# A macaron block on eight cores: the projection's loops are interchanged, and the softmax takes several PSUM banks per instruction

## The reference

```python
x = x + 0.5 * ffn(layernorm(x))
x = x + attn(layernorm(x))
x = x + 0.5 * ffn(layernorm(x))

def attn(x, Wkqv, bkqv, Wp, bp):          # 16 heads, D = 1024
    y = einsum('bnd,hde->bhne', x, Wkqv) + bkqv
    k, q, v = y[..., :1024], y[..., 1024:2048], y[..., 2048:]   # v has 64 columns
    A = einsum('bhnd,bhmd->bhnm', q, k) / sqrt(1024)
    A = softmax(where(causal, A, -inf))
    sa = einsum('bhnm,bhmd->bnhd', A, v).reshape(B, N, D)
    return sa @ Wp + bp
```

## Time and profile before

| | us |
|---|---|
| time, median of 2 runs | 8747.25 (8661.77 to 8832.72) |
| the profiled execution's own time | 8626.65 |
| its span, slowest core (core 4) | 8624.3 |
| TensorE matmul busy, core 4 | 5421.7 (63%) |
| TensorE weight load busy | 2495.0 (29%) |
| VectorE busy | 1917.7 (22%) |
| ScalarE busy | 1238.3 (14%) |

### The profile page before, as it was taken

How to read it: one execution, slowest core, us unless ns; L and a number is a source line. 1 busy time by engine, 2 the same in 40 slices (tenths; PEclk the granted TensorE clock), 3 DMA queues, 4 the chain that set the end, 5 groups by cost and what they waited for, 6 DMA issues and landing times.

```text
span 8624.3 us, 68745 instructions; the slowest of 8 cores (8527.9 to 8624.3 us)
## 1 busy us (share of the span) xinstructions
PE 5421.7 (63%) x24192; PEld 2495.0 (29%) x24192; DVE 1917.7 (22%) x4042; ACT 1238.3 (14%) x2572; POOL 176.0 (2%) x231
## 2 busy tenths in 40 slices
PE   4466465685766757667576675766757755446555
PEld 2122122232333323333233232332323322112222
DVE  2112121222221222222222222222222221210220
ACT  1112110111111111111111111111111111100110
POOL 0000000000000000000000000000000000000000
PEclk9677677776777868778688786887878877767777
DMA  3311313010101101011010010100101002322122
GB/s 68 56 23 36 59 20 52 11 21 0 21 5 16 18 3 21 5 16 21 1 21 10 11 21 1 21 10 11 21 0 21 1 1 90 72 50 33 38 46 42
DMA packets 170432, 213.87 MB, mean 25 GB/s; under 512 B 20816, under 2 KB 154224, under 8 KB 167792
## 3 DMA queue, kind: packets, MB, share of 16 engines
q0 software_dynamic: 154192, 155.24, 12.5%
q1 hardware_dynamic: 15904, 54.25, 1.8%
HBM read 339.49 MB, written 25.17 MB: 42 GB/s over the span
## 4 chain that ended last, share of the span: by engine, by line
PE 60%; DVE 15%; DMA 10%; issue 7%; ACT 6%; DVEq 1%; ACTq 0%; POOLq 0%; SPq 0%
PE psF L645 23%; PE psF L725 16%; PE psF L415 8%; PE psF L379 5%; ACT Pst L756 5%; DVE stat L743 5%; DMA f2b<-f 3%; PE psF L807 3%; DMA f2a<-f 3%; DVE PTs L791 2%; PE psT L786 2%; DVE Pst L777 2%; DVEq L74 1%; PE psF L336 1%; DMA f1b<-f 1%
## 5 line engine op out<-in xcount | busy, mean ns | idle before, releaser
L645 PE MATMUL psF<-ln_fm,wsl 128*128 128x512 bf16 x8704 | 1945.9, 388 | 41.7 <-DMA wsl<-wkqv 41.7
L725 PE MATMUL psF<-Kb,Qb 128*128 128x512 bf16 (+3 forms) x5120 | 1366.6, 439 | 0.0
L786 PE MATMUL psT<-ident,Pst 128*128 128x128 bf16 x2176 | 297.0, 300 | 1602.8 <-DVE Pst L777 1558.7
L645 PEld LDWEIGHTS psF<-ln_fm,wsl 128*128 128x128 bf16 x8704 | 870.5, 100 | 1112.2 <-issue 210.7
L725 PEld LDWEIGHTS psF<-Kb,Qb 128*128 128x128 bf16 x5120 | 570.7, 119 | 720.4 <-issue 463.5
L786 PEld LDWEIGHTS psT<-ident,Pst 128*128 128x128 bf16 x2176 | 198.6, 130 | 1755.1 <-issue 1755.1
L756 ACT ACTIVATE Pst<-psF,stat 128x512 bf16<-128x512 f32 (+3 forms) x640 | 398.7, 623 | 2122.4 <-DVE stat L747 2085.5
L668 ACT ACTIVATE Qb<-psF,bkqvq_sb 128x512 bf16<-128x512 f32 x512 | 351.7, 687 | 1423.6 <-PE psF L645 1423.5
L415 PE MATMUL psF<-mhb,f2b 128*128 128x512 bf16 x1024 | 350.5, 519 | 324.8 <-DMA f2b<-f 316.9
L415 PE MATMUL psF<-mha,f2a 128*128 128x512 bf16 x1024 | 347.6, 516 | 325.5 <-DMA f2a<-f 317.6
L657 DVE TENSOR_SCALAR Kb<-psF,bkqv_sb 128x512 bf16<-128x512 f32 x512 | 384.5, 751 | 630.2 <-PE psF L645 630.2
(11 more groups left out here) (106 smaller groups left out, 2252.0 us busy)
## 6 DMA issues: line engine op xcount, KB each, us to landing
wsl<-wkqv POOLq DMA_DIRECT2D x64, 1024.0 KB, 9.4
f2a<-f POOLq DMA_DIRECT2D x64, 512.0 KB, 5.3
f2b<-f POOLq DMA_DIRECT2D x64, 512.0 KB, 5.3
f1a<-f POOLq DMA_DIRECT2D x8, 1024.0 KB, 11.3
xta<-x SPq DMA_DIRECT2D x4, 2048.0 KB, 8.3
xs<-xta SPq DMA_DIRECT2D x4, 2048.0 KB, 6.5
x1t<-xs SPq DMA_DIRECT2D x4, 2048.0 KB, 9.1
xs<-x1t SPq DMA_DIRECT2D x4, 2048.0 KB, 7.6
```

What stands on the lines that cost most here:

```text
L645: outap=outap, ts=ts: e.matmul(outap, wsl[g][:, gw * c + 128 * jj: gw * c + 128 * jj + ofw], ln2_fm[:, 2048 * c + 512 * ts: 2048 * c + 512 ...
L725: lambda e, c=c, i=i, kw=kw, st=st, qb=qb: e.matmul(bank(st[i], kw), Qb[:, 2048 * c + 128 * qb: 2048 * c + 128 * (qb + 1)], Kb[:, 2048 * c ...
L786: (lambda e, col, i2=4 * tg + q, par=par: e.transpose(psT[:, col: col + 128], Pst[par][:, 128 * i2: 128 * (i2 + 1)], ident[:]))
```

## The change

Three edits, all in `build_program`:

1. In the projection, c is now the outer and ts the inner loop: the four banks are filled together, four matmuls in turn have the same weights, and the last matmul of each bank stands among the last four of the 32. One wait, at the first matmul of the tile, now names all four banks with their evictions in tile j-1, and only the last of the 32 matmuls counts up sT. The four evictions are written behind it.
2. The maximum (L743) and the exponential (L756) are taken over spans of several banks: one span of the whole W for even qb and for odd qb with W up to 1536, two spans (banks 3 to 5, and bank 0) for odd qb with W above 1536.
3. Where there is one span, its maximum is written negated straight into the column that the exponential reads, and its row sum straight into the column that the reciprocal reads: L747 and L767 are left out. The reciprocal waits for ScalarE as well.

```diff
-                        for ts in range(4):
-                            w = [("sW", wdone[g]),
-                                 ("sS", bankS[ts]), ("sV", bankV[ts])]
-                            if h == 0 and j == 0 and ts == 0:
-                                w += entry2
+                        w = [("sW", wdone[g])]
+                        for ts in range(4):
+                            w += [("sS", bankS[ts]), ("sV", bankV[ts])]
                             if j > 0:
                                 w.append(ev[(j - 1, ts)])
-                            for c in range(8):
+                        if h == 0 and j == 0:
+                            w += entry2
+                        for c in range(8):
+                            for ts in range(4):
...
-                                         waits=w if c == 0 else [],
-                                         inc="sT" if c == 7 else None)
-                            mmj = sch.cnt["sT"]
+                                         waits=w if (c == 0 and ts == 0) else [],
+                                         inc="sT" if (c == 7 and ts == 3) else None)
+                        mmj = sch.cnt["sT"]
+                        for ts in range(4):
...
+                    if par == 0:
+                        pieces = [(0, 0, W)]
+                    else:
+                        pieces = [(0, 1536, min(W, 1536))]
+                        if W > 1536:
+                            pieces.append((1536, 0, W - 1536))
+                    npc = len(pieces)
+                    if npc == 1:
+                        sch.emit("vector", lambda e, pc=pieces[0], par=par: e.reduce_max(
+                            stat[:, 26 + par: 27 + par],
+                            psF[:, pc[1]: pc[1] + pc[2]], AX, negate=True), inc="sV")
...
+                    for idx, pc in enumerate(pieces):
+                        acc = (smx[:, 8 + 2 * par: 9 + 2 * par] if npc == 1
+                               else smx[:, 4 * par + idx: 4 * par + idx + 1])
                         sch.emit("scalar",
...
+                                     psF[:, pc[1]: pc[1] + pc[2]], AF.Exp,
                                      bias=stat[:, 26 + par: 27 + par],
-                                     accum_out=smx[:, 4 * par + i: 4 * par + i + 1]),
+                                     accum_out=acc),
...
+                    if npc > 1:
+                        sch.emit("vector", lambda e, npc=npc, par=par: e.reduce_sum(
...
-                        waits=[("sV", ls_mark)], inc="sV")
+                        waits=[("sV", ls_mark), ("sS", expall)], inc="sV")
```

More of the change, by code:

```diff
@@ L632, in build_program @@
                         ofw = min(128, gw - 128 * jj)
+                        w = [("sW", wdone[g])]
                         for ts in range(4):
-                            w = [("sW", wdone[g]),
-                                 ("sS", bankS[ts]), ("sV", bankV[ts])]
-                            if h == 0 and j == 0 and ts == 0:
-                                w += entry2
+                            w += [("sS", bankS[ts]), ("sV", bankV[ts])]
                             if j > 0:
                                 w.append(ev[(j - 1, ts)])
-                            outap = (bank(ts) if ofw == 128
-                                     else psF[0:64, 512 * ts: 512 * ts + 512])
-                            for c in range(8):
+                        if h == 0 and j == 0:
+                            w += entry2
+                        for c in range(8):
+                            for ts in range(4):
+                                outap = (bank(ts) if ofw == 128
+                                         else psF[0:64, 512 * ts: 512 * ts + 512])
                                 sch.emit("tensor",
@@ new lines, in build_program @@
+                    npc = len(pieces)
[3 more added lines that the diff above has]
+                            psF[:, pc[1]: pc[1] + pc[2]], AX, negate=True), inc="sV")
+                    else:
+                        for idx, pc in enumerate(pieces):
+                            sch.emit("vector", lambda e, pc=pc, idx=idx: e.reduce_max(
+                                stat[:, 20 + idx: 21 + idx],
+                                psF[:, pc[1]: pc[1] + pc[2]], AX), inc="sV")
+                        sch.emit("vector", lambda e, par=par, npc=npc: e.reduce_max(
+                            stat[:, 26 + par: 27 + par], stat[:, 20: 20 + npc], AX,
+                            negate=True), inc="sV")
@@ L751, in build_program @@
                     mxd = sch.cnt["sV"]
-                    order = [3, 0, 1, 2] if nb == 4 else list(range(nb))
-                    for i in order:
-                        kw = min(512, W - 512 * i)
+                    for idx, pc in enumerate(pieces):
+                        acc = (smx[:, 8 + 2 * par: 9 + 2 * par] if npc == 1
+                               else smx[:, 4 * par + idx: 4 * par + idx + 1])
                         sch.emit("scalar",
-                                 lambda e, i=i, kw=kw, st=st, par=par: e.activation(
-                                     Pst[par][:, 512 * i: 512 * i + kw],
-                                     bank(st[i], kw), AF.Exp,
+                                 lambda e, pc=pc, par=par, acc=acc: e.activation(
+                                     Pst[par][:, pc[0]: pc[0] + pc[2]],
+                                     psF[:, pc[1]: pc[1] + pc[2]], AF.Exp,
@@ L763, in build_program @@
                                  inc="sS")
-                        exp_piece[(h, qb, i)] = sch.cnt["sS"]
-                        bankS[st[i]] = sch.cnt["sS"]
-                    expall = sch.cnt["sS"]
[L767 to L770, removed]
+                        mkpc = sch.cnt["sS"]
+                        for i in range(nb):
+                            cb = 512 * st[i]
+                            if pc[1] <= cb < pc[1] + pc[2]:
+                                exp_piece[(h, qb, i)] = mkpc
+                                bankS[st[i]] = mkpc
+                    expall = sch.cnt["sS"]
+                    if npc > 1:
+                        sch.emit("vector", lambda e, npc=npc, par=par: e.reduce_sum(
+                            smx[:, 8 + 2 * par: 9 + 2 * par],
+                            smx[:, 4 * par: 4 * par + npc], AX),
+                            waits=[("sS", expall)], inc="sV")
                     ls_mark = sch.cnt["sV"]
```

## The result

The changed kernel takes 9717.8 us (median of 11 runs, 9657.6 to 9770.8) against 8684.5 us of the kernel before in the same comparisons (10 runs). The ratio is 1.131, with an interval of 1.125 to 1.137: slower by 13%.

The account below looks back on a forecast made before the run. It took TensorE's matmuls and the serial softmax chain as what bounds the slowest core. 8627 + 929 + 358 - 44 - 366 = 9504 us, put at 9520, 8.8% above the median; range 9180 to 9790 us.

Parts of the forecast that it names:

- Part 1: Projection: TensorE stands still for four evictions, 3.62 us after K tiles, 3.32 after Q, 2.55 more at V; +929 us.
- Part 2: Projection matmuls behind the new pauses: lower granted clock, 1.4 us in each of 256, +358 us (bounds 0 to 589).
- -44 us: Projection of the first three heads: the held-down clock of 0.81 to 0.91 would go; other end 0.
- rival C: Projection: clock lost as behind the 6.2 us pauses, 2.3 us in each, 9751 us in all; chance 0.17.
- Part 3: Softmax: merged maxima and exponentials save fixed costs and hand-overs, 22.9 us in a head, -366 us (bounds -366 and 0).
- Part 4: Weight loads, next weights' DMAs and fewer sT counts in the projection: no change in time, 0 us.
- Rival B: Projection: weights used four times drop three of four loads, 653 us less, 8493 us with full clock; chance 0.04.
- Rival A: Projection: the clock holds through the pauses, 9162 us in all; chance 0.17.
- Rival D: Softmax: maxima and exponentials over several banks gain nothing, 9886 us in all; chance 0.04.

Follow-up runs that it names:

- the softmax part alone: The changed kernel with the projection's loops put back as before, wider maxima and exponentials kept; 8151.2 and 8156.4 us, ratio 0.949 to the kernel before.
- the fills: The changed kernel with 14, 8 or 4 unused matmuls behind each K and Q tile; 9131.6 to 9251.5, 9125.8 and 9157.2, and 9244.0 us.
- pairs: The changed kernel with two banks filled at a time, one wait and one count for 16 matmuls; 8169.2 and 8169.4 us.
- 8 fill matmuls: The changed kernel with 8 matmuls of unread result added behind each K and Q tile; 9125.8 and 9157.2 us.
- 4 fill matmuls: The changed kernel with 4 matmuls of unread result added behind each K and Q tile; 9244.0 us in the one comparable execution.

## Why the prediction was right in kind and too small in size

**Part 1, the wait.** Right. The pauses are 3.65 and 3.33 us (3.62 and 3.32), those before K and Q tiles 898.5 us in all (8 x 3.62 and 8 x 3.32 in 16 heads are 888), and V's is 3.73 us. That nothing would hide them is shown by the idle time of the group.

**Part 2, the clock.** This is the step that failed: "I take 1.4 us, nearer the long pause", with -44 us for the clock that had been held down. Together they put 314 us on the matmuls of the projection; 514 us came, 200 too few, and that is the 196 us by which the sum missed. The other terms miss by 20 us or less and nearly cancel. Against bursts at full clock (1895.7 us, the softmax part alone) the changed kernel loses 564 us, 2.2 us in each of 256 tiles, practically the 2.3 us of the earlier trace rows. So rival C was right about the size of this term. The mistake was to interpolate between the pauses of the earlier trace rows by their length, and to read the mean clocks of 0.86 and 0.82 there as losses of a part. Cut more finely, the row of 0.82 behind the pause of 2.90 us is 1.00 for 1.8 us and then 0.50:

```profile
1361.60:1363.40 1.80, 0.93 (x12) 0.61 (x12) 1.20 (x2) 0.00 (x0) 0.00 (x0) 1.00 0.00 0
1363.60:1366.60 3.00, 2.24 (x16) 1.39 (x16) 2.58 (x4) 0.00 (x0) 0.00 (x0) 0.50 0.00 0
```

A single pause either leaves the burst behind it at 7.07 us or little more, or costs it 1.3 us at the least: 1.7 us in the bursts of 8.75 us, 2.8 us in that of 9.86 us. What the term needed was how many of the 256 bursts are hit, nearly all of them here (11 of 257 escape), and no row of the kernel before could tell that. The -44 us didn't come either. In the changed kernel the clock of 0.81 is there too, within the burst that starts at 5314.65, between two pauses:

```profile
5319.50:5324.50 5.00, 5.00 (x20) 1.85 (x17) 0.00 (x0) 0.00 (x0) 0.00 (x0) 0.81 0.00 0
```

Pauses for a third of the time don't keep it away, as part 2 had assumed. The fall behind pauses is shown by the fills; how much of the 564 us is at 0.81 and how much at 0.50 was not separated by a run.

**Part 3, wider instructions.** Right. 2158 and 1862 ns were forecast as 2.16 and 1.86 us, and the softmax part alone saves 25.4 us in the head shown (22.9). Four maxima and four exponentials are one each there, so crossing three bank boundaries had no price that these numbers show. In the changed kernel the same stage saves 21.0 us, of which V's evictions take 2.55; 23.6 without them.

**Part 4, edits at nothing.** Right. Weights used in turn don't speed up the matmuls: 1896.1 us with pairs against 1895.7 without. One reading was slightly off: the 28 loads in 5.93 us start 216 ns apart, and not 212, since the last one's own 0.1 us is in the 5.93. Rival B falls with it, and so does the 131 ns that the Trainium skill, "TensorE: Matmul & The Clock Gate", section "Back-to-back issue gap", gives for a matmul of 512 columns: the runs show 217.8 ns (1895.7 us for 8704). Fewer counts of sT brought nothing either, as the trace had said: pairs have half the counts and the same busy time.

Rival A, a clock that holds, was wrong for these pauses. It describes the kernel with 8 fill matmuls, at 9126 us and near its 9162, but not the one with pauses of 2.15 us. Rival D is excluded by the durations.

The forecast's base added to the miss in per cent. It was 8747.25 us, the median of two executions, while the ratio of 1.131 puts the kernel before at 9717.8 / 1.131 = 8592 us. Against 8747.25 us the changed kernel's 9717.8 us are 11.1% more and inside the range. That the time in us lies inside is therefore no sign that part 2 was well sized: the range held rival C, and its upper end is 72 us away.

## What to carry to other kernels

When a loop is interchanged so that all of its PSUM banks finish together, count the banks that the next tile can use meanwhile: with none, every eviction stands on the path, and reused weights don't pay for it, since the loads were hidden. Price a new pause of TensorE twice, once for its length and once for the burst behind it. Read the granted clock behind such pauses in fine stretches and over many of them: a mean of 0.82 can be a full fall that came late, and what counts in the sum is how often it comes. Merging small instructions on a serial chain over several banks saved their fixed costs and hand-overs in full here, and can be taken without such a loop change.

## What the runs showed of the hardware that was not expected

- Behind pauses of one length a burst of 32 matmuls takes either 7.1 to 7.3 us or, with few between, 8.3 us and more; what changes between the kernels is how many are hit. Full clock kept 11 of 257 bursts behind 3.65 and 3.33 us, 102 of 257 behind 2.15 us (evictions on two engines), 172 of 257 behind about 2.8 and 2.5 us with 4 fill matmuls before them, and 254 of 256 behind 1.9 and 1.60 us with 8. So the length of the pause alone doesn't order the losses. What the stream does around the pause matters too; in what way, no run here tells.
- More work made the kernel faster: 3584 useless matmuls took 466 us or more off the changed kernel's time.
- A pause that waits for two engines was longer than its evictions by 2.15 - 1.61 = 0.54 us, one that waits for VectorE alone, in the changed kernel, by 3.65 - 3.33 = 0.32 us. The cause was not tried.
